# Softmax of a windowed attention: the maximum given to ScalarE as the bias of ten exponentials

## The reference, cut to what matters

```python
attn = jnp.einsum('whid,whjd->whij', q, k) * HEAD_DIM ** (-0.5)
bias = rpb[REL_IDX].transpose(2, 0, 1)
attn = attn + bias[None]
...                                         # the second block adds a mask of the window
attn = jax.nn.softmax(attn, axis=-1)        # over the 49 keys: exp(s - max) / sum
out = jnp.einsum('whij,whjd->whid', attn, v)
```

## Time and profile before

| what | us |
|---|---|
| median of 3 runs | 3116.05 (3107.86 to 3117.09) |
| the profiled execution | 3117.1 |
| its span in the trace | 3115.6 |
| PE busy | 2991.0 (96%) |
| DVE busy | 2226.9 (71%) |
| ACT busy | 1715.5 (55%) |
| POOL busy | 843.7 (27%) |

### The profile page before, as it was taken

How to read it: one execution, slowest core, us unless ns; L and a number is a source line. 1 busy time by engine, 2 the same in 40 slices (tenths; PEclk the granted TensorE clock), 3 DMA queues, 4 the chain that set the end, 5 groups by cost and what they waited for, 6 DMA issues and landing times. The chain is left out here.

```text
span 3115.6 us, 102843 instructions
## 1 busy us (share of the span) xinstructions
PE 2991.0 (96%) x39898; PEld 2698.7 (87%) x39898; DVE 2226.9 (71%) x6736; ACT 1715.5 (55%) x4076; POOL 843.7 (27%) x1470
## 2 busy tenths in 40 slices
PE   7889999999999999999999999999999999999689
PEld 5678888898888888888888898889888988898589
DVE  5767777777777777777777777777777777777322
ACT  5456656656665566565655555555555555555121
POOL 8122222222222222222233223322332233222111
PEclk9989999999999999999999999999999999999799
DMA  6421111111111111111111111111111111111484
GB/s 141 147 65 40 37 34 39 36 29 39 39 39 39 39 39 32 38 41 50 37 41 35 31 32 39 38 31 29 39 39 32 27 39 39 33 26 27 84 145 83
DMA packets 210424, 147.29 MB, mean 47 GB/s; under 512 B 15954, under 2 KB 205205, under 8 KB 210331
## 3 DMA queue, kind: packets, MB, share of 16 engines
q1 hardware_dynamic: 207619, 142.41, 19.6%
q10 hardware_dynamic: 1008, 3.44, 0.5%
q0 software_dynamic: 1728, 0.48, 0.1%
HBM read 95.64 MB, written 52.50 MB: 48 GB/s over the span
## 5 line engine op out<-in xcount | busy, mean ns | idle before, releaser
L1503 PE MATMUL rm<-w,ht 128*112 128x160 f32 x4480 | 682.9, 302 | 0.0
L1503 PEld LDWEIGHTS rm<-w,ht 128*112 128x112 f32 x4480 | 611.9, 177 | 5.3
L989 POOL TENSOR_TENSOR rs<-ln_tmp,mhalf 112x4 f32<-112x4 f32 (+1 forms) x128 | 119.3, 932 | 1622.9 <-DVE ln_tmp L1161 1622.8
L1079 ACT ACTIVATE ht<-rm 128x448 f32<-128x448 f32 (+1 forms) x640 | 319.1, 499 | 193.6 <-PE rm L122 193.6
L1044 ACT ACTIVATE vb<-ra 113x320 f32<-113x320 f32 x256 | 113.1, 442 | 278.4 <-PE ra L122 276.8
L122 PE MATMUL rm<-z2t_hi,w_hi 128*128 128x448 f32 (+1 forms) x640 | 257.8, 403 | 4.4 <-DVE z2t_rest L1269 3.3
L947 POOL TENSOR_TENSOR z<-z,one 112x448 f32<-112x448 f32 (+2 forms) x192 | 131.6, 685 | 348.6 <-DVE z L1165 348.6
L122 PE MATMUL rm<-z2t_rest,w_rest 98*128 98x448 f32 (+1 forms) x640 | 219.7, 343 | 0.0
L122 PE MATMUL rm<-z2t_lo,w_hi 128*128 128x448 f32 (+1 forms) x640 | 219.3, 343 | 0.0
L122 PE MATMUL rm<-z2t_hi,w_lo 128*128 128x448 f32 (+1 forms) x640 | 218.0, 341 | 0.0
L1208 DVE TENSOR_TENSOR sc<-so,tabs 113x490 f32<-113x490 f32 x256 | 171.3, 669 | 56.0 <-PE so L1449 43.6
(11 more groups left out here) (253 smaller groups left out, 8868.3 us busy)
## 6 DMA issues: line engine op xcount, KB each, us to landing
xa<-xs SPq DMA_DIRECT2D x128, 245.0 KB
xr<-xs SPq DMA_DIRECT2D x128, 245.0 KB
xs<-xo SPq DMA_DIRECT2D x64, 245.0 KB
ys<-yz SPq DMA_DIRECT2D x64, 245.0 KB
c_y<-ys SPq DMA_DIRECT2D x48, 260.0 KB
xs<-a_tok SPq DMA_DIRECT2D x14, 560.0 KB, 6.4
xs<-tok_late SPq DMA_DIRECT2D x14, 560.0 KB, 6.8
c_y<-ys SPq DMA_DIRECT2D x16, 280.0 KB
```

The source lines that it names most:

```text
L989: gp.tensor_tensor(rs[1][:, t0:t0 + nt], ln_tmp[1][5][:, t0:t0 + nt], mhalf[:, 0:nt], ALU.pow).then_inc(s_pow, 1)
L1079: act_(ht[:, f * SN + t0 * TT:f * SN + (t0 + nt) * TT], bank_m(i, lm, use)[:, 0:nt * TT], ACT.Gelu_apprx_tanh).then_inc(m_freed(i, lm, use ...
L1503: last = mm(bank_m(i, lm, use)[0:TT, t * DIM:(t + 1) * DIM], ht[:, c:c + TT], keep.w["w2", lm][:, f * DIM:(f + 1) * DIM], start=(f == 0), ...
```

## The change

DVE writes the biased scores straight to `sm` (the tile `sc` is gone) and reduces them as before. In place of the subtraction over 490 columns it negates the ten maxima into a small tile `less`, one of two. ACT takes one exponential for each of the ten blocks of 49 columns, each with its column of `less` as bias; only the last signals. The wait for `exps(j - 2)`, which protects the buffers, moves from the subtraction up to the addition. PE and POOL keep their instructions.

```diff
-        sc = sb("sc", [QP, HEADS * GK])
         mx = sb("mx", [QP, 2 * HEADS])
+        less = [sb(f"less{n}", [QP, 2 * HEADS]) for n in range(2)]
...
                 def exps(j):
                     act.wait_ge(s_ssub, i * NG + j + 1)
-                    act_(view(pr[j % 2], 0, QP, 0, [[WP, 2 * HEADS], [1, WT]]), view(sm[j % 2], 0, QP, 0, [[WT, 2 * HEADS], [1, WT]]),
-                         ACT.Exp).then_inc(s_exp, 1)
+                    for g in range(2 * HEADS):
+                        last = act_(pr[j % 2][:, g * WP:g * WP + WT], sm[j % 2][:, g * WT:(g + 1) * WT], ACT.Exp,
+                                    bias=less[j % 2][:, g:g + 1])
+                    last.then_inc(s_exp, 1)
...
                     reach(dve, s_ssub, n - 1)
-                    v.tensor_tensor(view(sc, 0, QP, 0, [[SX, 2], [1, SX]]), view(so, 0, QP, 0, [[512, 2], [1, SX]]), tab,
+                    reach(dve, s_exp, n_ * NG + j - 1)
+                    v.tensor_tensor(view(sm[j % 2], 0, QP, 0, [[SX, 2], [1, SX]]), view(so, 0, QP, 0, [[512, 2], [1, SX]]), tab,
                                     ALU.add).then_inc(s_sadd, 1)
...
-                    s3 = sc[:].rearrange("q (g k) -> q g k", k=WT)
+                    s3 = sm[j % 2][:].rearrange("q (g k) -> q g k", k=WT)
                     v.tensor_reduce(mx[:], s3, AX.X, ALU.max).then_inc(s_smax, 1)
                     dve.wait_ge(s_smax, n)
-                    reach(dve, s_exp, n - 2)
-                    v.tensor_tensor(sm[j % 2][:].rearrange("q (g k) -> q g k", k=WT), s3,
-                                    view(mx, 0, QP, 0, [[1, 2 * HEADS], [0, WT]]), ALU.subtract).then_inc(s_ssub, 1)
+                    v.tensor_scalar(less[j % 2][:], mx[:], -1.0, None, ALU.mult).then_inc(s_ssub, 1)
```

## The result

| | before | after |
|---|---|---|
| median of 4 runs, us | 3116.29 (3107.86 to 3117.09) | 3395.37 (3393.57 to 3397.25) |
| ratio, 95% interval | 1 | 1.0903 [1.0885, 1.0921] |
| span of the profiled execution, us | 3115.6 | 3395.7 |

The change costs 279 us. The forecast was 3380, range 3275 to 3470.

What follows compares the result with a forecast made beforehand. PE, busy 96% of the span, was taken to bound the kernel. ACT's longer exponentials add 32 x 4.5 + 32 x 3.7 = 262 us to 3117.1, making 3379, stated as 3380 us; range 3275 to 3470.

Steps and rivals of the forecast that it cites:

- The mechanism: ACT's longer exponentials make PE wait at four places in a strip; DVE's saving and its moved wait cost nothing.
- the 0.2 at most: DVE's group 0.5 us shorter; about 0.2 would reach PE through `outputs(0)`, 12 us at most, if ACT were no later.
- The step: ACT's time from one 49-column exponential to the next: 0.235 us, from fixed part, per-partition operand and columns.
- The first pair: ACT's `queries` with a per-partition operand takes 591 ns, `keys` of the same shape 505: 0.09 us for the operand.
- The walk: One strip followed through the queues: 4.5 us longer in layer 0, 3.7 in layer 1.
- 1. `weights_turned(0)`: PE waits for `exps(0)`, ending at 1002.76: begins at 1002.82 instead of 1001.80, 1.0 us late.
- Step 2: PE's `outputs(0)` waits for ACT's copy of `pt`: starts at 1006.55 instead of 1003.83, 2.7 us late.
- 3. Q0, layer 0: PE's Q0 waits for DVE's split behind `exps(2)` and `front_hi(1)`: starts at 1010.38 instead of 1006.86, 3.5 us late.
- 4. `weights_turned(3)`, layer 0: PE waits for `exps(3)`: begins at 1013.38 instead of 1012.36, 1.0 us more; sum 4.5 us a strip.
- The moved wait: DVE's addition of group 2 now waits for `exps(0)`; hidden behind ACT, costed at nothing.
- PEclk still 1.00: Sign: PE's granted clock stays full, with 2991 of 3379 us busy (89%).
- the rival: PE's clock falls to 0.89 throughout because of its standstills: 360 us more, 3740 us; chance 4%.

Runs made afterwards that it cites:

- ACT's work alone: Kernel before with ten exponentials of 49 columns, each with a bias column of zeros; DVE and its waits unchanged: 3396.07 us, ratio 1.0906.
- the moved wait alone: Kernel before with only DVE's wait for `exps(j - 2)` moved from the subtraction to the addition: 3108.82 us, ratio 0.9987.
- one exponential for a group: Changed kernel with one maximum for the whole row of 490 and one exponential with one bias column: 3110.29 us, ratio 0.9986.
- ten without bias: Kernel before with ten exponentials of 49 columns and no per-partition operand; DVE still subtracts, no wait moves: 3176.9 us, ratio 1.0192.
- groups 0 and 1: Kernel before with ten exponentials and a bias of zeros only in `exps(0)` and `exps(1)`: 3333.35 us, ratio 1.0693.
- the other order: Changed kernel, same instructions, with `exps(1)` moved behind `weights_out(0)` and `exps(2)` behind `outputs_hi(0)` in ACT's queue: 3321.61 us, ratio 1.0662.
- the filled kernel: Changed kernel with seven useless products ahead of PE's wait in `outputs(0)`: 3378.65 us, ratio 1.0854.
- five: Kernel before with five exponentials of 98 columns (two blocks each) and a bias column of zeros; DVE as before: 3174.99 us, ratio 1.0181.
- group 3 alone: Kernel before with ten exponentials and a bias of zeros only in `exps(3)`: 3179.12 us, ratio 1.0197.
- The filled kernels: Useless products ahead of PE's wait in `outputs(0)`: changed kernel with twelve, 3395.09 us, or seven, 3378.65; ten biased pieces in `exps(0)`, `exps(1)` only, with twelve, 3332.03.

## Why the prediction was right, and where it was not

**The mechanism** holds. ACT's work alone is the whole loss, the moved wait alone is nothing, and DVE's relief, with one exponential for a group, is 0.19 us in a strip of layer 0, which is the 0.2 at most that the prediction named.

**The step.** Forecast 0.235, measured 0.227. (The terms of the forecast, 0.10 + 0.09 + 0.041, add up to 0.231, not 0.235.) Both parts were measured by themselves: without the operand 0.134, of which 49 columns are 0.041 and 0.093 is fixed (forecast 0.10), and 0.093 for the operand (forecast 0.09). The first pair, copies of `queries` and `keys`, had been the right rows for it. The Trainium skill, "Perfetto Trace Analysis", section "Optimizing Scalar/DVE Operations", gives about 93 ns of overhead for an instruction of ScalarE on SBUF. The runs agree with it where there is no operand, and show that a bias column adds as much again.

**The walk**, in us behind the start of `exps(0)`:

| | before | forecast | measured |
|---|---|---|---|
| 1. `weights_turned(0)` | 1.50 | 2.52 | 2.43 |
| 2. `outputs(0)` | 3.53 | 6.25 | 6.35 |
| 3. Q0, layer 0 | 6.56 | 10.08 | 9.95 |
| 4. `weights_turned(3)`, layer 0 | 12.06 | 16.56 | 16.38 |
| sum, layer 0 / layer 1 | | 4.5 / 3.7 | 4.36 / 3.83 |

Step 2 is later than forecast though the exponentials were shorter. The copy of `pt` ended at 6.15, 0.04 before the forecast's 6.19; PE went on 0.20 behind its end, not 0.06. The sum of the short strips is 262 us, the forecast's to the last digit. That is luck: layer 0 had been put too high by 0.14 us a strip and layer 1 too low by 0.13. The prediction calls ACT's queue nearly full from 1000.30 to 1012.36; it was busy 9.35 of these 12.06 us, with holes of 1.03 and 0.87 us. The walk itself goes by start times and is not hurt by this.

**ACT's busy time** rose by 412, not by 460. The exponentials themselves grew by 447 (152.8 to 600.3); busy time counts overlapping instructions once. **DVE's** fell by 111, not by 128. The group itself fell as forecast, from 171.9 to 44.6 (174 ns for each `less`). The other 16 are not added work: with ACT's work alone DVE has the instructions of before and is busy for 2240.7 us instead of 2226.9. That this too is instructions which overlap less where DVE has to wait is likely, but was not shown. Neither is on the path.

**The moved wait** was costed at nothing. DVE does wait 1.66 us for it in every strip, and the kernel with ACT's work alone has the wait in its old place and is as slow, so PE does not feel it.

**The step that failed** is "PEclk still 1.00". It was argued from PE's mean load over the whole span, and so the rival gave the clock only one form, 0.89 throughout, at 360 us. What came is another: about a third of the strips get 1.2 GHz for some 3.4 us behind their two standstills. The mean load does not tell the kernels apart: PE is busy 92% of the span with groups 0 and 1, which has long strips, and 91% in the other order, which has none. In the changed kernel the falls cost 16 to 23 us (16 to 17 by the filled kernel, 23 by the strips' lengths), enough for the whole distance between the forecast 3380 and the measured 3395. In the kernel with groups 0 and 1 it is 42 us, most of the miss of that expectation. The walk also put the standstill ahead of `outputs(0)` at 1.7 us, where PE waited 1.9.

**Open.** Why some strips fall and others, with the same standstills, do not. PE's rows of a short and a long strip of layer 1 are alike up to the fall, and with groups 0 and 1 nearly every third strip of layer 1 is long, so chance it hardly is. What the runs say is that strips fall only in kernels with a standstill of 2.1 us in each strip, behind one of 0.9. Those whose regular standstills are at most 1.16 us (ten without bias, five, group 3 alone, the other order) show no long strip. The filled kernels keep the standstill of 0.9 and lose the one of 2.1, and have none either. So the long one is needed; whether it would do without the one of 0.9 ahead of it was not tried.

## What to carry to other kernels

The busy share of an engine says nothing of what added work on it costs: ACT was 55% busy, and 4 x 1.75 = 7.0 us more work in a strip of 41 made it 4.4 longer, the same 7.0 in another order only 3.2. Walk one strip queue by queue instead, from the instruction that grows to the next engine that waits. And before an operand is moved into an instruction for free, ask whether the instruction must be split for it: here ten pieces pay ten times the fixed 0.09 us and ten times the 0.09 of the operand, while one maximum for the whole row, which softmax allows, needs one piece and keeps all of the gain there was (0.19 us in a strip of layer 0, some 6 us in all; the times, 0.14% faster, can't tell it from nothing).

## What the runs showed of the chip

- A bias column costs an exponential 90 ns whatever its size: 711 against 621 at 490 columns, 330 against 237 at 49. It doesn't overlap with the instruction ahead (steps of 0.227 and 0.134).
- TensorE's clock fell to 1.2 GHz for some 3.4 us behind two standstills of which the longer was only 2.1 us. This cost 0.7 to 1.7 us each time. It is seen in the strips' lengths and in windows of 2 us; the mean clock shows it too, but as little as 0.984 against 0.974.
- Useless products in such a standstill gave back 16 us. Each of these fp32 products of 128 columns of weights took two loads: twelve were too many (2.78 us in a hole of 2.11) and seven fitted (1.67).
